# Cross-attention and a routed FFN on one core: the output bias is added to the next block ahead of the four scatters

## The reference

```python
x = x + xattn(layernorm(x), ctx_1024, Wq, bq, Wk, bk, Wv, bv, Wo, bo)   # 16 heads of 16, 128 keys a batch
x = x + ffn(layernorm(x), router_w, router_b, weights1, bias1, weights2, bias2)

def ffn(x):                                  # 32 experts, hidden size 64
    e = argmax(x_flat @ router_w.T + router_b)
    y = relu(relu(x_flat @ w1[e] + b1[e]) @ w2[e] + b2[e])      # each token through one expert
```

## Time and profile before

| | |
|---|---|
| median of three executions | 1323.57 us (1322.7 to 1328.38) |
| the profiled execution | 1323.38 us, its span 1321.3 us |
| mean granted TensorE clock | 0.971 |
| busy: PE, PEld, DVE, ACT, POOL | 1146.4, 877.5, 941.1, 832.5, 854.2 us |
| attention phase | to about 1020 us of the span |
| GpSimd in `add_bo` | 32 instructions |
| GpSimd in the block scatters | 128 instructions |

### The profile page before, as it was taken

One profiled execution on the slowest core, in us unless ns is written; L12 is line 12 of the kernel. 1 busy time (PEld: TensorE's weight loads), 2 busy tenths in 40 slices (PEclk: granted clock), 3 DMA queues, 4 the chain that ended last, 5 costly groups with the idle time before them and its releaser, 6 DMA issues.

```text
span 1321.3 us, 38981 instructions
## 1 busy us (share of the span) xinstructions
PE 1146.4 (87%) x15015; PEld 877.5 (66%) x15015; DVE 941.1 (71%) x2449; ACT 832.5 (63%) x1892; POOL 854.2 (65%) x1613
## 2 busy tenths in 40 slices
PE   5999999999999999999999999999986087777775
PEld 4777777777777777777777777777764076666664
DVE  3788887788787888888778878788774155555554
ACT  3677776777777777777677777777763044444443
POOL 4535767767667777677776766777555656666555
PEclk8999999999999999999999999999998599999999
DMA  8315223422222222222222222221102245555540
GB/s 253 108 51 116 78 68 99 120 75 66 74 67 65 71 69 66 71 78 70 76 83 67 67 74 67 66 74 54 34 23 92 93 139 177 173 166 167 153 113 19
DMA packets 89235, 120.37 MB, mean 91 GB/s; under 512 B 12176, under 2 KB 71963, under 8 KB 88861
## 3 DMA queue, kind: packets, MB, share of 16 engines
q1 hardware_dynamic: 75230, 84.03, 22.5%
q0 software_dynamic: 13824, 33.85, 7.0%
HBM read 60.61 MB, written 59.31 MB: 91 GB/s over the span
## 4 chain that ended last, share of the span: by engine, by line
PE 53%; DVE 31%; issue 6%; ACT 4%; POOL 2%; DMA 1%; another core or an unknown queue 1%; DVEq 1%; SPq 0%; POOLq 0%; ACTq 0%
DVE mx L574 14%; PE pB L804 11%; PE pA L757 8%; PE pB L811 5%; PE sc L965 4%; PE sc L764 4%; PE m L973 3%; DVE tr L598 3%; PE sc L956 3%; PE sc L786 3%; DVE nrm L602 3%; PE m L773 3%; DVE row L583 3%; PE sc L795 2%; PE pA L748 2%
## 5 line engine op out<-in xcount | busy, mean ns | idle before, releaser
L574 DVE TENSOR_REDUCE mx<-m 128x4 bf16<-128x512 f32 x512 | 324.0, 673 | 53.3 <-PE m L773 53.0
L452 ACT ACTIVATE arena<-sc 128x512 f32<-128x512 f32 x512 | 264.5, 603 | 37.0 <-PE sc L795 23.1
L403 POOL DMA_INDIRECT out<-arena x160 | 159.7, 998 | 108.7 <-DVE arena L722 71.3
L786 PE MATMUL sc<-qk 32*128 32x256 f32 x2048 | 167.5, 397 | 0.3
L374 POOL DMA_INDIRECT pages<-row,slot_i x128 | 132.1, 1032 | 49.2 <-issue 32.2
L804 PE MATMUL pB<-arena 128*32 128x128 f32 x4096 | 147.7, 277 | 13.6 <-DVE row L583 0.5
L598 DVE STREAM_TRANSPOSE tr<-pB 128x512 f32<-128x512 f32 x128 | 91.8, 718 | 84.7 <-PE pB L804 74.2
L533 ACT ACTIVATE arena<-sc 128x256 f32<-128x256 f32 x160 | 61.3, 383 | 137.2 <-PE sc L956 87.2
L811 PE MATMUL pB<-wo_s,aT 128*128 128x256 f32 x512 | 138.6, 393 | 4.4 <-DVE aT L607 4.4
L804 PEld LDWEIGHTS pB<-arena 128*32 128x32 f32 x4096 | 108.6, 110 | 36.2 <-DVE row L583 30.9
L786 PEld LDWEIGHTS sc<-qk 32*128 32x128 f32 x2048 | 115.5, 186 | 0.7 <-ACT arena L456 0.6
(11 more groups left out here) (145 smaller groups left out, 2717.4 us busy)
## 6 DMA issues: line engine op xcount, KB each, us to landing
arena<-pages SPq DMA_DIRECT2D x40, 520.0 KB
cT<-ctxT SPq DMA_DIRECT2D x64, 256.0 KB, 4.2
xs<-x_in SPq DMA_DIRECT2D x128, 128.0 KB, 2.1
pages<-empty SPq DMA_DIRECT2D x120, 130.0 KB, 3.0
pages<-empty SPq DMA_DIRECT2D x1, 5200.0 KB, 19.3
out<-arena POOLq DMA_INDIRECT x160
w2s<-w SPq DMA_DIRECT2D x1, 2080.0 KB
qk<-w SPq DMA_DIRECT2D x1, 2064.0 KB
```

The costliest lines, as they stand in the source:

```text
L403: pool.indirect_dma_start(out_rows, bass.IndirectOffsetOnAxis(pr[:, r, COL_TOKEN:COL_TOKEN + 1].bitcast(U32), 0), pr[:, r, 0:D], None, bou ...
L452: act.activation(pt[:, u % 2, g].rearrange("p i k -> p (i k)"), sc[g][:, :], ACT.Exp).then_inc(S["exp_out"], 1)
L574: ins = dve.tensor_reduce(mx[:, 32 * g:32 * g + 4], mb[i][:, :].rearrange("p (h k) -> p h k", h=4), AX.X, ALU.max)
L786: pe.matmul(dst, kT[rows, q % 2, c, u * P:(u + 1) * P], qM[rows, q % 2, :, c, u * P:(u + 1) * P], start=(c == 0), stop=False, skip_group_c ...
```

## The change

`add_bo(s + 1)` is called ahead of `scatter(s - 3)` in an iteration of GpSimd's loop, where it was called behind it. Nothing else differs.

```diff
                 if live(s - 1):
                     rstd2(s - 1, 1)
+                if live(s + 1):
+                    add_bo(s + 1)
                 if live(s - 3):
                     scatter(s - 3)
-                if live(s + 1):
-                    add_bo(s + 1)
                 if live(s - 2):
                     meta(s - 2)
                     fresh_pages(s - 2)
```

## The result

| | before, same chip | after |
|---|---|---|
| median | 1324.78 us (4 executions) | 1415.47 us (4 executions, 1409.31 to 1422.32) |
| ratio | | 1.0657, 95% interval 1.0607 to 1.0707 |
| profiled execution | 1323.38 us, span 1321.3 | 1409.62 us, span 1407.7 |
| mean granted TensorE clock | 0.971 | 0.918 |

The change costs 6.6%, about 87 us. I had forecast 1355 us, and the range ended at 1376. The direction was right, the size was not.

What follows compares the result with a forecast made beforehand. TensorE (53% of the chain) and VectorE (31%) were taken to bound the kernel, GpSimd 2%. First slot +1.17 us, second -0.06, +1.11 a block, times 28 = +31 us on 1323.38: forecast 1355 us, range 1335 to 1376.

Steps and rivals of the forecast that it cites:

- `eq` beside the addition: First slot (u=1 to 2): VectorE's `eq` grows from 0.30 to 1.47 us beside the moved addition, +1.17 us a block.
- `nrm` set free: Second slot (u=2 to 3): VectorE's `nrm`, no longer beside the addition, falls from 0.81 to 0.46 us, 0.35 us off.
- The third term: Second slot: with later scatters `tr` starts 3.45 to 3.6 us behind the residual instead of 3.17; slot 8.57 us.
- Rival B: Second slot: `tr` stays 1.84 us behind the fourth scatter's start, the hold-up grows, +2.04 us a block, 1380.5 us; chance 0.10.
- Rival C, the clock: TensorE's idle behind `eq` lowers its clock: 1386 us if every block pays, about 1370 if every second; chance 0.17.
- Rival A, the hold-up goes: Second slot: TensorE's results no longer held, slot down to 6.87 us, -0.59 us a block, 1307 us; chance 0.10.

Runs made afterwards that it cites:

- e3: Kernel before, with the addition moved behind the split of the context, ahead of the second half of rstd2; 1318.15 us.
- e10: Changed kernel with a GpSimd memset of 700 words of an unused tile between one scatter and the next; 1323.47 us.
- e15: Changed kernel with a GpSimd memset of 250 words of an unused tile between one scatter and the next; 1366.03 us.
- e2: Changed kernel with the bias addition replaced by a GpSimd memset of an unused tile of about the same length; 1347.05 us.
- e7: Kernel before without its four scatters a block and with the addition behind the split of the context; 1253.77 us, with a shorter page part.
- e6: Changed kernel with the four indirect scatters replaced by plain GpSimd DMAs of the same rows to consecutive page rows; 1307.17 us.
- e9: e5 with the addition where the changed kernel has it, directly behind rstd2 and ahead of the slot cast; 1319.01 us.
- e4: Kernel before without its four scatters a block, the addition then falling beside `eq`; 1299.78 us, with a shorter page part.
- e1: Changed kernel with two float32 matmuls of zeros put on TensorE where it idles for the maxima in pass u=2; 1370.88 us.
- e14: Changed kernel with a GpSimd memset of 16 words of an unused tile between one scatter and the next; 1414.2 us.
- e5: e3 with a block's four scatters taken apart: behind the slot cast, meta, fresh_pages and the next iteration's first rstd2; 1282.16 us.
- e8: e3 with all four scatters, unbroken, moved behind fresh_pages; 1346.0 us.

## Why the prediction was wrong

- `eq` beside the addition: right, +1.17 us expected in the first slot, 1.15 in the usual block (8.52 - 7.37), 32.5 us over all `eq` instructions.
- `nrm` set free: right here. It was freed (-10.4 us in its group), and from `tr` to the next residual it is 5.08 us where I had 5.11. That this needs a late `tr` I had not seen: in e3 the same 0.35 us are lost.
- The third term was mis-sized. I took `tr` at 3.45 to 3.6 us behind the residual, from iteration 31, whose fourth scatter stood nearly as late (2.64 us). It came at 4.00. I had passed over the scatters ahead of that fourth one. In iteration 31 before:

```profile
989.94 1.21 POOL L374 DMA_INDIRECT pages<-row,slot_i  x1 [0.51 <-POOL slot_i L370]
994.47 0.99 POOL L374 DMA_INDIRECT pages<-row,slot_i  x1 [3.31 <-issue]
```

So there only three scatters follow each other closely, in the kernel after four. That this made the row too cheap fits e10 and e15, where the distance decides, but no run shows it by itself. The fourth scatter came at 650.61 - 648.37 = 2.24 us, 0.3 earlier than I had put it, and `tr` 1.76 behind it. Rival B's distance of 1.84 held in this kernel, though e2 shows that it isn't a rule. Price of the step: second slot 9.08 instead of 8.57, 0.51 x 28 = 14 us.
- Rival C, the clock, was real, and it is the larger part of the miss. The step that failed is to take its price as mostly hidden behind the hold-up. I gave it 0.17, "mostly as every second block" at 1.06 us. Low clock came in 23 of 28 blocks and cost 1.0 to 2.3 us in each, 36 us in all. The price was in my rows: 1.86 us in iteration 2. Of these 0.35 were the routing work that iteration 1 lacks (7.22 without scatters in e7, not 6.87); the other 1.5 are what a fall costs in e6, e9 and e10, and 36.4 / 23 = 1.6 is the mean in the kernel after. I took the cheaper row of iteration 31. In the kernel after the price came on top of the hold-up.
- Nor did the hold-up make the falls rarer. The idle of about 1.5 to 1.8 us without it brought the low clock in 2 to 7 of 28 blocks (e4, e6, e9, e10), the hold-up with 0.39 to 0.67 us of idle in 0 to 7 (before, e3, e2, e1), both together in 23 and 27 (after, e14), and in 16 where the hold-up was shorter (e15). Why a given block falls stays open. In the block shown TensorE has gaps of 0.45 and 0.42 us ahead of L757, 2 to 3 us behind the wait of 1.54, but the spared block before it has the same wait (1.53) and gaps (0.45 and 0.44).
- Rival A, the hold-up goes, did not happen, but the prize it named is there: e5 has the second slot at 7.22 us (A had 6.87, the slot of iteration 1, which has no routing).

Sum: 1355 + 14 (hold-up) + 36 (clock) = 1405 against the profiled 1409.6. Of the remainder 3.5 us lie behind the last residual (310.0 against 306.5), where nothing was changed; kernels that share this part differ there from 301 to 311 us.

What stays open is what in an indirect scatter holds TensorE's results. The runs show that it goes with the indirect form (or what e6 changed with it), that it piles up when scatters start less than about 2 us apart, and that GpSimd's own small instructions in between don't matter.

## What to carry to other kernels

Read a GpSimd instruction by what it reads and what it stands beside, not by its busy share: here 2.4 us of addition cost 1.15 us on VectorE in one place and nothing in another. Don't issue indirect scatters back to back in a phase in which others wait for TensorE; taken apart between other GpSimd work they cost 0.2 us a block here, not 1.4 (1282 us in e5, 1318 in e3). And where a change opens an idle gap on TensorE in every block, price the clock in full from a row at hand, and for every block: one idle that brings the low clock in a few blocks by itself brought it in most of them together with the held results.

## What the runs showed that I had not expected

- Four indirect scatters in a row cost 1.4 to 2.3 us of a block (second slot 8.64 and 9.08 against 7.22, third slot 9.92 in e8 against 7.60); plain DMAs of 128 rows, four in 2.32 us, cost nothing.
- 2.1 us of useless memsets a block on GpSimd bought 91 us (1414.2 us in e14, with the same instructions at 16 words, 1323.5 in e10; one execution each).
- With the idle alone, low clock came at regular distances, every fourth or fifth block (e6, e10); in the kernel after it came in nearly every block, at 1.0 to 1.2 us in the first after a spared one and 1.4 to 2.3 in the next ones.
